# Causal mask of the scores moved from TensorE to VectorE, half masks in the maximum pass, and new orders in an attention and expert layer

## The reference

```python
xn = layernorm(x)                       # x: (4, 1024, 256) f32
q, k, v = heads(xn @ Wq), heads(xn @ Wk), heads(xn @ Wv)    # 16 heads of 64
sim = einsum('bid,bjd->bij', rope(q), rope(k)) * 64 ** -0.5
attn = softmax(where(tril(ones(1024, 1024)), sim, -inf))
att = (attn @ v).reshape(4, 1024, 1024) @ Wo + bo
# 32 experts: each takes its 8 best tokens of 1024 of every batch, merges them with
# its gates to one, runs 257 -> 1024 -> gelu -> 257 -> 256, and adds the result back
out = x + att + experts(xn)
```

## Time and profile before

| | |
|---|---|
| median of 3 runs | 1419.1 us (1415.09 to 1420.23) |
| profiled execution | 1423.84 us, span 1422.0 us |
| mean granted TensorE clock | 0.984 |
| PE busy | 1350.8 us (95%), 11556 matmuls |
| POOL busy | 974.1 us (68%) |
| DVE busy | 897.5 us (63%) |
| ACT busy | 631.3 us (44%) |
| last chain of work, share by engine | PE 83%, DMA 5%, ACT 4%, DVE 3%, issue 3% |
| mask matmuls in scores (L1320) and maxima (L1338) | 1024 and 1024 of 128 columns |

### The profile page before, as it was taken

The page is one execution under the profiler, slowest core; times in us unless marked ns, Lnnn a source line. Parts: engine busy times, 40 slices in busy tenths (PEclk is TensorE's granted clock), DMA queues, the critical chain, the costliest instruction groups (busy, mean ns, idle before and its releaser), DMA issues.

```text
span 1422.0 us, 31224 instructions
## 1 busy us (share of the span) xinstructions
PE 1350.8 (95%) x11556; PEld 880.9 (62%) x11556; DVE 897.5 (63%) x1186; ACT 631.3 (44%) x954; POOL 974.1 (68%) x662
## 2 busy tenths in 40 slices
PE   6799999989899999999999999999999999999989
PEld 5465666655556555556676776666666776666647
DVE  5778777845666566666346766666667666666631
ACT  3355565542444445434324444454444444444430
POOL 2566677755665676566566776888789768888861
PEclk9799999999999999999999999999999999999999
DMA  5314233575678667864641321212232222212111
GB/s 175 113 68 157 93 118 135 183 247 193 224 272 282 226 208 246 274 231 159 180 153 54 94 79 57 80 65 76 86 107 91 68 81 93 76 62 76 46 50 60
DMA packets 123712, 189.78 MB, mean 133 GB/s; under 512 B 29680, under 2 KB 58768, under 8 KB 123568
## 3 DMA queue, kind: packets, MB, share of 16 engines
q1 hardware_dynamic: 93136, 113.42, 23.8%
q10 hardware_dynamic: 30384, 74.23, 15.4%
q0 software_dynamic: 48, 0.13, 0.1%
HBM read 131.63 MB, written 22.54 MB: 108 GB/s over the span
## 4 chain that ended last, share of the span: by engine, by line
PE 83%; DMA 5%; ACT 4%; DVE 3%; issue 3%; SPq 1%; POOL 0%; ACTq 0%; POOLq 0%; DVEq 0%
PE t_pO L1410 17%; PE t_pF L1385 12%; PE t_pA L1308 9%; PE t_pF L1368 7%; PE t_pB L1308 6%; PE t_pA L1332 3%; PE t_pC L1332 3%; PE t_pA L1313 2%; PE t_pC L1419 2%; PE t_pB L1313 2%; PE t_pB L1470 2%; DMA t_swap<-t_raw 2%; PE t_pC L1470 2%; PE t_pB L1460 2%; PE t_pC L1460 2%
## 5 line engine op out<-in xcount | busy, mean ns | idle before, releaser
L701 POOL TENSOR_TENSOR t_acc<-t_acc,t_PT 128x1024 f32<-128x1024 f32 (+3 forms) x256 | 438.9, 1715 | 168.7 <-ACT t_PT L772 149.4
L1410 PE MATMUL t_pO<-t_PT,t_V 128*64 128x512 f32 (+3 forms) x1536 | 293.2, 503 | 9.4 <-issue 5.0
L676 POOL TENSOR_TENSOR t_swap<-t_swap,t_sin 128x512 f32<-128x512 f32 x124 | 164.7, 1329 | 194.5 <-DMA t_swap<-t_raw 194.5
L772 ACT ACTIVATE t_PT<-t_pA 128x1024 f32<-128x1024 f32 x192 | 169.7, 884 | 270.1 <-PE t_pA L1320 233.0
L1385 PE MATMUL t_pF<-t_xT,t_wqk 128*128 128x512 f32 x756 | 212.5, 417 | 5.5 <-issue 3.8
L1410 PEld LDWEIGHTS t_pO<-t_PT,t_V 128*64 128x64 f32 x1536 | 94.4, 137 | 149.3 <-issue 127.2
L679 POOL TENSOR_TENSOR t_rot<-t_rot,t_swap 128x512 f32<-128x512 f32 x124 | 178.0, 1436 | 9.8 <-POOL t_swap L676 0.2
L1385 PEld LDWEIGHTS t_pF<-t_xT,t_wqk 128*128 128x128 f32 x756 | 134.4, 191 | 46.7 <-issue 14.1
L1036 DVE TENSOR_TENSOR t_LO<-t_rot,t_HI 128x512 fp32r<-128x512 f32 x124 | 156.0, 1258 | 7.5 <-ACT t_HI L804 7.5
L794 ACT ACTIVATE t_raw<-t_pF 128x512 f32<-128x512 f32 x124 | 74.0, 597 | 169.1 <-PE t_pF L1385 147.1
L772 ACT ACTIVATE t_PT<-t_pB 128x768 f32<-128x768 f32 (+1 forms) x192 | 142.0, 739 | 13.4 <-PE t_pB L1320 11.1
(11 more groups left out here) (206 smaller groups left out, 2417.8 us busy)
## 6 DMA issues: line engine op xcount, KB each, us to landing
t_w1t<-in_L_ffn_w ACTq DMA_DIRECT2D x32, 1024.0 KB, 5.9
t_w2t<-in_L_ffn_w ACTq DMA_DIRECT2D x32, 1024.0 KB, 8.7
t_swap<-t_raw SPq DMA_DIRECT2D x248, 128.0 KB, 2.1
t_OT<-r_s SPq DMA_DIRECT2D x128, 128.0 KB, 2.9
t_wqk<-wqk_s SPq DMA_DIRECT2D x24, 512.0 KB, 3.4
xt_s<-t_xs SPq DMA_DIRECT2D x6, 1024.0 KB, 5.2
t_xT<-xt_s ACTq DMA_DIRECT2D x6, 1024.0 KB, 6.4
t_wvs<-wv_s SPq DMA_DIRECT2D x12, 512.0 KB, 3.8
```

The costliest lines, as they stand in the source:

```text
L676: pool.tensor_tensor(swap_of(r), swap_of(r), sin[:, c * BANK:(c + 1) * BANK], ALU.mult).then_inc(sin_sem, 1)
L701: pool.tensor_tensor(a[:, :, off:], a[:, :, off:], pt, ALU.add).then_inc(acc_done, 1)
L772: act.activation(PT[:, n % PTS, :, 0:w], bank[:, :, 0:w], ACT.Exp, scale=SCALE).then_inc(exp_done, 1)
L1410: mm = pe.matmul(pO[h * DH:(h + 1) * DH, off:], v, PT[:, n % PTS, h, 0:w], start=(j == 0), stop=(j == 4 * c + 3))
```

## The change

- The four mask matmuls of a diagonal chunk's scores go. VectorE instead multiplies the diagonal 128 columns of both heads' exps by 0 or 1 (`cut`; the min with 3e38 takes infinities away first). The values and GpSimd's additions wait for it (`cut_done`). In a VectorE stage the cut of the first chunk stands ahead of the first maximum and that of the second chunk behind it.
- In the maximum pass each mask matmul streams 64 columns and writes half of the diagonal tile.
- Batch 3's output is split: `part` multiplies pairs 0 to 6 of the batch (21 fp32r matmuls) and the expert term in stages (31, 1) to (32, 2), `keep` adds x and the bias; `last` adds pair 7 in one f32 matmul behind its normalisation, `finish` adds and two tiles are stored at a time.
- VectorE inverts behind the rope and normalises at the stage's end; SP stores the reciprocal behind the swap. In stage 2 of the expert pairs TensorE puts the fill between the two maximum banks. The first output tile of y = 0 goes behind the values.
- In the prologue ScalarE takes the first two exps ahead of other copies, with a small exp first that loads the table; the moments' statistics move by some stages.

```diff
+            def cut(P, c, j):
+                n = chunk_index(P, c, j)
+                if on_diagonal(c, j):
+                    dve.wait_ge(exp_done, n + 1)
+                    dve.scalar_tensor_tensor(PT[:, n % PTS, :, 0:P128], PT[:, n % PTS, :, 0:P128], -USED,
+                                             allowed[:, :].unsqueeze(1).to_broadcast([P128, 2, P128]),
+                                             ALU.min, ALU.mult).then_inc(cut_done, 1)
...
             for s, (P, g) in enumerate(STAGES):
-                n = normalise_of(*STAGES[s - 2]) if s >= 2 else None
-                if n is not None:
-                    invert(n)
                 pair, banks = maxima_of(P, g)
+                chunks = chunks_of(P, g)
+                for chunk in chunks[:1]:
+                    cut(*chunk)
                 for m, pieces in enumerate(banks):
                     maximum(pair, MAXES[P, g] + m, (pC, pA)[m % 2], pieces)
+                    if m == 0:
+                        for chunk in chunks[1:]:
+                            cut(*chunk)
+                if not banks:
+                    for chunk in chunks[1:]:
+                        cut(*chunk)
...
                 if fill_of(P, g) in ROPE:
                     rope(fill_of(P, g))
+                n = normalise_of(*STAGES[s - 2]) if s >= 2 else None
+                if n is not None:
+                    invert(n)
                 n = normalise_of(*STAGES[s - 3]) if s >= 3 else None
-                if n is not None:
+                if n is not None and P == N:
                     normalise(n)
...
+                n = normalise_of(*STAGES[s - 3]) if s >= 3 else None
+                if n is not None and P < N:
+                    normalise(n)
...
             # GpSimd, accumulate
                 pool.wait_ge(exp_done, n + 1)
+                pool.wait_ge(cut_done, CUT[P, c, j])
...
             # TensorE, scores
-                if diag:
-                    for r in range(2):
-                        for h in range(2):
-                            d = slice(h * DH, (h + 1) * DH)
-                            z = (h + r) % 2
-                            mm = pe.matmul(bank[:, h, 0:P128], maskk[d, r, :], maskq[d, r, :], start=False, stop=(r == 1))
...
             # TensorE, maximum
+                            half = slice(at + w - P128 + r * DH, at + w - P128 + (r + 1) * DH)
                             for h in range(2):
                                 d = slice(h * DH, (h + 1) * DH)
-                                mm = pe.matmul(bank[:, h, at + w - P128:at + w], maskq[d, r, :], maskk[d, r, :],
-                                               start=False, stop=(r == 1))
+                                mm = pe.matmul(bank[:, h, half], shifted(maskd, d, r), maskq[d, :], start=False, stop=(r == 1))
...
             # TensorE, values
                 pe.wait_ge(exp_done, n + 1)
+                pe.wait_ge(cut_done, CUT[P, c, j])
...
+            def part(t):
...
+                for k in range(PAIRS - 1):
+                    for o, hw in ((oh, 0), (oh, 1), (ol, 0)):
+                        pe.matmul(bank, o[:, t % 2, k, :], woh[:, hw, k, :], start=(a == 0), stop=False)
+                        a += 1
+                pe.wait_ge(moe_loaded, B * 80)
+                pe.matmul(bank, wsp[:, t * P128:(t + 1) * P128], oe[:, :], start=False, stop=True).then_inc(y_part, 1)
+
+            def last(t):
...
+                pe.wait_ge(o_done, 2 * (N - 1) + t // 4 + 1)
+                pe.matmul(out_bank(t), OT[:, PAIRS - 1, t * P128:(t + 1) * P128], wlast[:, :],
+                          start=True, stop=True).then_inc(y_mm, 1)
...
             # TensorE, stages
+                after_gelu = g == 2 and 0 <= P - MOE < E // GE
                 for m, pieces in enumerate(banks):
+                    if m == 1 and after_gelu and fill_of(P, g):
+                        fill(fill_of(P, g))
...
             # SyncE, stages
-                n2 = normalise_of(*STAGES[s - 2]) if s >= 2 else None
-                if n2 is not None:
-                    store_recip(n2)
                 f = fill_of(P, g)
...
+                n2 = normalise_of(*STAGES[s - 2]) if s >= 2 else None
                 if n is not None:
                     load_sums(n)
                 if n2 is not None:
+                    store_recip(n2)
                     spread_recip(n2)
```

183 lines of the change are left out of this document (135 added, 48 removed).

## The result

The changed kernel takes 1473.0 us (median of 4 runs, 1469.5 to 1473.5) against 1419.7 for the kernel before beside it: ratio 1.0362, 95% interval 1.0331 to 1.0392. It is 53 us slower, where 13 were forecast.

A forecast was written before the change was run, and what follows sets the result against it. TensorE was taken as the bound (busy 95% of the span). Terms 35 + 2 + 1 - 13 - 2 - 2 - 5 - 3 = +13 us took the median from 1419.1 to 1432 us, range 1385 to 1470.

The forecast's parts named there:

- late pairs: Pairs 18 to 23, 26 to 30: +3.2 us each, +35 in all; +2.2 of each from TensorE's wait in stage 1.
- part 2: Cut on VectorE: 256 operations, 0.41 us each free, up to 2.4 us more behind GpSimd; late pairs +35 us in all.
- A: The forecast itself: late pairs lengthen by 2 to 4 us, 1426 to 1450 us; chance 0.38.
- Part 1: Scores' mask leaves TensorE: 256 groups of 0.17 us, 44 us gained if TensorE never waits for the new work.
- Part 3: Half masks in the maximum pass: 2 us gained, between nothing and 12; 0 by the skill's rule for loads.
- Part 4: Fill between the maxima in experts' stage 2: -1.0 us x 8, -13 with stage 1's 0.6; first output tile -2.
- Part 5: Split tail: 34 us behind the last sums becomes 16.5, pair 31 gains 15 us of work; net -5, bounds -10, +3.
- Part 6: Prologue: exps ahead of two copies remove a 3.2 us wait; -3 us, bounds -7 and +2.
- D: Rival: pairs 1 to 13 lose 2.5 us each, second scores waiting behind stage 0's rope; +32 us, 1465 us; chance 0.14.
- B: Rival: late pairs cost 0, cuts slipping in ahead of GpSimd's rope; -22 us, 1397 us; chance 0.26.
- C: Rival: TensorE gets all the gains, the cut never waiting for GpSimd; 1345 us, or 1357; chance 0.10.
- E: Rival: late pairs lengthen by about 1.5 us and the parts cancel, 1412 to 1426 us; chance 0.12.

The follow-up runs named there:

- a_nocut: Changed kernel without its cut, both mask passes on TensorE with full 128 columns, all else kept: 1424.5 us, ratio 1.0028 to the kernel before.
- a_late: Changed kernel with the first query half's normalisation moved from the end of stage 5 to the end of the next pair's stage 0: 1468.7 us, ratio 1.0334.
- b_cut: Kernel before with the cut on VectorE in place of the scores' masks and half masks in the maximum pass, old orders kept: 1458.3 us, ratio 1.0276.
- b_cut_free: b_cut with GpSimd's additions of the exps cut to 8 columns of each head, sums left incomplete: 1413.7 us, ratio 0.9944.
- b_cut_small: b_cut with the cut over 2x8 columns for 2x128, same place and waits, rest of the diagonal tile unmasked: 1422.9 us, ratio 1.0056.
- b_half: Kernel before with every mask matmul streaming 64 columns for 128, in scores and maxima: 1410.3 us, ratio 0.9928.
- b_gelu: Kernel before with one edit, TensorE's fill between the two maximum banks in stage 2 of the expert pairs: 1421.5 us, ratio 1.0018.
- a_nocut_late: a_nocut with half masks in both passes and the first query half's normalisation at the end of the next pair's stage 0: 1402.3 us, ratio 0.9884.

## Why the prediction was wrong

- **The sum.** +13 forecast, +53 measured; slower was right, the size not, and 1473 lies above the range's end of 1470. What made it too small isn't the late pairs, on which most of the working was spent, but two terms that had a sentence or two each: pairs 7 to 13 come out 33 us over their forecast of 7 x -1.6 us, pairs 1 to 5 20 us over theirs. It is luck that the total isn't further off: the late pairs' term was 23 us too high, and pair 6 won 10 us more than forecast.
- **Pairs 1 to 5, "+1 us in all": +21.5.** Their longer stages were taken for room. VectorE was already busy for 75% of that stretch before, with statistics and reads of x, and in a_nocut the loss is gone. How it splits into named waits stays open in part: 5.3 us for the bank reads, 6.1 us of values behind cuts, 9.0 us that stand as "issue", and 4.0 us of longer busy time at the lower clock.
- **Pairs 6 to 13, "leaves VectorE room": +21.8 in pairs 7 to 13.** I had worked out in part 2 that the normalisation comes late, and priced it only in late pairs. Beside the experts' transfers its spread takes 6.7 to 9.1 us from issue to landing, where it takes 3.4 to 4.6 in late pairs, and its store 2.6 to 5.2 us, for 1.4 to 2.7. So it lands 3.5 to 6.1 us into stage 0, not 1.6, and the wait stands ahead of both maxima. (Before, it took 5.6 to 9.3 us as well, but was issued some 8.7 us ahead of stage 0.) a_late, which moves the normalisation alone, takes 26.5 us off, a_nocut, which takes the cut away and keeps the late spread, 13.0: a cut behind the wait makes it longer, and the two shares don't add up.
- **Late pairs, +3.2 us each: +0.9 (18 to 23) and +1.4 (26 to 30),** 12 us for 35. Stage 4 came out as worked out: second cut to 5.5 us (5.52), maximum to 6.65 (6.66), next scores at 6.7 (6.71). Stage 5 is 4.8 to 4.9, for 5.05, and the spread lands 1.5 us into stage 0 (median), for 1.6. The step that fails there is stage 1: the wait of its fill for the rope (+2.2 us). In eight of the eleven pairs the rope of stage 0 ends 6.8 to 7.5 us in, not 10.4, because the low part and the combine get in ahead of GpSimd's next instruction. Stage 1 is 3.96 us in the median, at the edge of what I had named as a sign of being wrong (under 4). In pair 28 the chain comes out as worked out: combine behind the swap's multiply, rope until 9.8 us, and stage 1 takes 6.64 us for 3.87:

```profile
1303.33 1.23 DVE L1095 TENSOR_TENSOR t_nm<-t_nma,t_nmb 128x8 f32<-128x8 f32 x1
...
1305.26 2.32 PE L1492 MATMUL t_pF<-t_xT,t_wqk 128*128 128x512 f32 x6 [1.56 <-issue]
```

In b_cut, where the normalisation is early, the rope ends at 8.5 and the fill of stage 1 begins at 1.74 for 1.37: the chain is there in nine of the eleven pairs, but stage 1 grows by 0.4 to 0.5 us, not 2.2.
- **Turns with GpSimd: right in kind.** Free 0.43 us (0.41 said), at most 2.5 (2.8), mean 0.81, below the 0.9 given for A. b_cut_free (7 us for 40) shows that the loss needs these turns; b_cut_small (6 us, with the waits kept) adds what the prediction hadn't, that it needs VectorE's own time as well.
- **Part 1's price.** 0.17 us a group was high: the first exp of stage 0 ends at 2.26 us for 2.40, 0.13 us a group (0.10 by the start of the next scores), 34 us in all for 44.
- **Part 3, -2 us (0 to -12).** b_half: 10 us for 512 groups, so some 5 us for these 256, inside the bounds. The Trainium skill (TensorE: Matmul & The Clock Gate, "LDWEIGHTS (loading the stationary operand)") has a load's time go by its columns; had the loads alone set the group's time, the part would have been 0. The weights keep their 128 columns and the group is shorter all the same, so here the columns streamed count.
- **Part 4, -8 us of the -13.** The covered wait (ScalarE behind the Gelu) wasn't the one that ends the stage: b_gelu gives nothing. It is the reciprocal's load. With the reciprocal moved too, the stage wins 1.5 us. The first output tile fits: stage 1 of pair 14 is 9.9 us for 12.2.
- **Part 5, -5 us** (its own terms add up to -4.3): nothing measurable. 23.7 us are left for the 16.5 worked out, since VectorE serves parts ahead of the last reciprocal.
- **Part 6, -3 us:** -4.0 in the trace, but the stretch up to pair 1 is between -7.4 and +5.0 in kernels with either start; it can't be told.
- **The rivals.** D had the time (1465) and the place (pairs 1 to 13), with another mechanism: a read of the expert bank behind the rope. Its kind of wait is there (5.3 us for t_xs in pairs 1 to 5) and is a quarter of that stretch's loss. B (late pairs at 34.7 us or so) and C (33.3) fell: all eleven are 35.2 us or longer, and 35.5 or longer in b_cut. A, the forecast itself, fell with them (2 to 4 us a late pair). E had the late pairs best (about 1.5 us for the measured 0.9 and 1.4) and the total wrong.

## What to carry over

Before work goes to another engine, read that engine's busy share in each stretch, not over the span: where it was at 75%, 0.25 us less of work in each of 40 cuts took 10 us off that stretch (b_cut_small), its whole length. Beside a neighbour with which it takes turns the instruction can be held up too (107 of 256 were). If it has to go there, issue it once for two chunks rather than twice. A wait for a transfer belongs at a point of the queue behind which nothing is due soon, and moving it means asking what stands behind it in the stretch where transfers are slowest.

The fastest version is a_nocut_late: masks on TensorE with 64 columns streamed, the reciprocal behind the rope, the fill between the maxima behind the Gelu, and the normalisation at the end of stage 0. Half masks alone (b_half) give 10 of its 16 us.

## What the runs showed of the hardware

- VectorE and GpSimd take turns by whole instructions: 107 of the 256 cuts took over 0.1 us more than the median of 0.43 us, up to 2.5 us.
- The spread of a reciprocal, DRAM to SBUF, takes 3.4 to 4.6 us from issue to landing in late pairs and 6.7 to 9.1 us beside the experts' weight loads (changed kernel, pairs 7 to 13).
- A tensor_scalar with one fp32 SBUF input and an SBUF output waits for GpSimd like one with two inputs: 94 of 256 took over 0.1 us more than the median of 0.30 us, up to 2.2 us. My prediction had tied the waiting to two inputs. The Trainium skill (SBUF — State Buffer, "SBUF: two separate sides") names two cases for the lock, two SBUF inputs or a perf mode with two ports; by the second the trace agrees, though no run here shows which mode was chosen.
- The masking form takes 0.18 us for 16 columns, 0.43 for 256 and 0.68 for 512.
- A group of four mask matmuls costs 0.10 to 0.13 us with 128 columns streamed and some 0.02 to 0.04 less with 64. With 64 weight columns for 128, and 64 or 128 streamed, it is dearer: 0.05 us more up to the first exp of stage 0, 0.22 us up to the second.
